# Flamingo layer on one core: pads written ahead, row scatters one tile a step, eight heads' exponentials moved to ScalarE from PSUM

## The reference

```python
def reference(x, ctx, g_xattn, g_ffn, ...):            # x: 2 x 1024 x 256, ctx: 2 x 64 x 256
    q = (layernorm(x) @ Wq + bq) / sqrt(64)            # 16 heads of 64
    k, v = ctx @ Wk + bk, ctx @ Wv + bv
    a = softmax(q @ k.T) @ v                           # per head, 64 keys
    x = x + tanh(g_xattn) * (a @ Wo + bo)
    h = layernorm(x)
    s = sigmoid(h @ W_router)                          # 8 experts
    sel = top_k(s + expert_bias, 2)
    w = s[sel] / sum(s[sel])
    shared = silu(h @ Wg_s) * (h @ Wu_s) @ Wd_s
    routed = sum over the two experts e of w_e * (silu(h @ Wg[e]) * (h @ Wu[e]) @ Wd[e])
    return x + tanh(g_ffn) * (shared + routed)
```

## Time and profile before

| | before |
|---|---|
| median of 3 runs | 332.17 us (331.71 to 333.2) |
| the profiled execution | 331.99 us, its span 330.2 us |
| mean granted TensorE clock | 0.946 of full speed |
| busy: PE, DVE, ACT, POOL | 279.2, 248.5, 153.6, 160.6 us |
| transfers | 38.01 MB; SP's queue 27.13 MB |

### The profile page before, as it was taken

One profiled execution on the slowest core, in us unless ns is written; L12 is line 12 of the kernel. 1 busy time (PEld: TensorE's weight loads), 2 busy tenths in 40 slices (PEclk: granted clock), 3 DMA queues, 4 the chain that ended last, 5 costly groups with the idle time before them and its releaser, 6 DMA issues.

```text
span 330.2 us, 6385 instructions
## 1 busy us (share of the span) xinstructions
PE 279.2 (85%) x1724; PEld 251.2 (76%) x1725; DVE 248.5 (75%) x708; ACT 153.6 (47%) x387; POOL 160.6 (49%) x208
## 2 busy tenths in 40 slices
PE   3968979999989989969968779089799999999680
PEld 2958768999979978959957667078699999999560
DVE  1696898999999998869967755028877777777666
ACT  1362455555555654635433365024456555555310
POOL 7022023355556888884788505705644443444400
PEclk9997999999999999998979999659999999999877
DMA  5792003011111232342003992232344334334668
GB/s 189 264 338 64 0 0 97 1 50 49 50 49 45 77 113 75 96 129 66 32 34 118 319 287 75 81 93 84 96 114 124 101 103 125 118 112 128 203 222 287
DMA packets 33628, 38.01 MB, mean 115 GB/s; under 512 B 3816, under 2 KB 30274, under 8 KB 33602
## 3 DMA queue, kind: packets, MB, share of 16 engines
q1 hardware_dynamic: 28018, 27.13, 27.7%
q0 software_dynamic: 3408, 8.46, 7.5%
q10 hardware_dynamic: 2176, 2.10, 1.9%
HBM read 21.67 MB, written 16.93 MB: 117 GB/s over the span
## 4 chain that ended last, share of the span: by engine, by line
PE 43%; DVE 18%; POOL 12%; issue 12%; DMA 6%; SPq 5%; ACT 2%; DVEq 0%; POOLq 0%; ACTq 0%
POOL rows_dram L556 6%; PE bank L1232 5%; PE scores_ps L1232 4%; PE bank L1233 4%; PE bank L1234 4%; PE scores_ps L1233 4%; PE scores_ps L1234 4%; DMA x_sb<-in_x_dram 3%; PE bank L1389 3%; POOL probs L585 2%; PE bank L1218 2%; DVE pT_lo L1032 2%; DVE row_sum L1037 2%; DMA routed_dram<-probs,sct_idx 2%; DVE probs L1061 2%
## 5 line engine op out<-in xcount | busy, mean ns | idle before, releaser
L638 POOL DMA_INDIRECT routed_dram<-probs,sct_idx x39 | 38.6, 991 | 56.2 <-ACT probs L804 55.1
L585 POOL TENSOR_TENSOR probs<-probs,row_inv 128x1024 f32<-128x1024 f32 x16 | 30.5, 1906 | 33.9 <-DVE row_inv L1041 33.9
L556 POOL DMA_INDIRECT rows_dram<-xn,slot_i x32 | 31.9, 997 | 20.1 <-DMA rows_dram<-pad_rows 11.5
L1232 PE MATMUL bank<-AB_hi,pT_hi 128*128 128x256 f32 x128 | 38.5, 301 | 0.0
L1234 PE MATMUL bank<-AB_hi,pT_lo 128*128 128x256 f32 x128 | 37.0, 289 | 0.0
L1233 PE MATMUL bank<-AB_lo,pT_hi 128*128 128x256 f32 x128 | 37.0, 289 | 0.0
L1232 PE MATMUL scores_ps<-AB_hi,xnT_hi 128*128 128x512 f32 x64 | 25.9, 404 | 3.4 <-DVE xnT_lo L1021 3.4
L1120 DVE TENSOR_TENSOR xnT_lo<-bank,xnT_hi 128x256 fp32r<-128x256 f32 x39 | 16.5, 424 | 14.9 <-ACT xnT_hi L789 13.7
L719 ACT ACTIVATE probs<-probs 128x1024 f32<-128x1024 f32 x16 | 16.9, 1058 | 19.0 <-DVE probs L1061 19.0
L1232 PEld LDWEIGHTS bank<-AB_hi,pT_hi 128*128 128x128 f32 x128 | 25.6, 200 | 0.0
L1233 PEld LDWEIGHTS bank<-AB_lo,pT_hi 128*128 128x128 f32 x128 | 25.6, 200 | 0.0
(11 more groups left out here) (224 smaller groups left out, 864.2 us busy)
## 6 DMA issues: line engine op xcount, KB each, us to landing
rows_dram<-pad_rows SPq DMA_DIRECT2D x8, 650.0 KB, 10.6
probs<-rows_dram SPq DMA_DIRECT2D x30, 130.0 KB, 2.2
x_sb<-in_x_dram SPq DMA_DIRECT2D x2, 1024.0 KB, 9.7
AB_free<-routed_dram SPq DMA_DIRECT2D x4, 512.0 KB, 6.3
AB_free<-routed_dram SPq DMA_DIRECT2D x8, 256.0 KB, 4.8
out_dram<-x_sb ACTq DMA_DIRECT2D x8, 256.0 KB, 2.2
raw_buf<-in_L_ffn_Wg_dram SPq DMA_DIRECT2D x8, 192.0 KB, 2.5
raw_buf<-in_L_ffn_Wu_dram SPq DMA_DIRECT2D x8, 192.0 KB, 2.7
```

The source lines that it names most:

```text
L556: nc.gpsimd.indirect_dma_start(rows_dram[:, :], bass.IndirectOffsetOnAxis(ap=slot_i[:, t, k:k + 1], axis=0), xn2[:, t % KEEP, :], None).th ...
L585: nc.gpsimd.tensor_tensor(pr, pr, row_inv[:, :].unsqueeze(2).to_broadcast([P, H, KV]), ALU.mult).then_inc(norm_done, 1)
L638: nc.gpsimd.indirect_dma_start(routed_dram[:, :], bass.IndirectOffsetOnAxis(ap=sct_idx[(k - 2) % (2 * RING)][:, 0:1], axis=0), y_sb[ks][:, ...
L1232: nc.tensor.matmul(out_ap, a_hi, b_hi, start=first, stop=False)
```

## The change

1. **Pads ahead.** Every region is now exactly 16 tiles (`REGION = T`) and is filled with pads as a whole before rows are scattered over them: the first 6 tiles of each of the 8 regions right behind the loads (`fill_first`), and one more tile of all regions with each later weight transfer (`fill_next`). Pool waits for the fill that covers the tile it scatters. Counting for the pads, `put_pads` and their semaphores are gone.
2. **Scatters.** Pool scatters one tile in each step from 6 on, right behind the second norm and ahead of the normalising; tile 9 at the end of step 14, tiles 10 and 11 in step 15.
3. **Batches** are (0,3), (3,6), (6,9), (9,12) and then as before; `rank` stands behind the scores on TensorE and `place` behind the subtraction on VectorE.
4. **Softmax.** Scores are made negative by the sign of the query weights, the maximum becomes a minimum, and for heads 0 to 7 ScalarE takes exp(-s + min) straight from PSUM with the sum in the same instruction, one instruction for each head. Heads 8 to 15 go as before, at half the width.
5. **ScalarE's order.** The experts' weight copy comes before the transposed second tile, the direct exponentials after it, Wd's copy after those; xnT_hi comes ahead of the old exponential.

```diff
-REGION = T + 1
+REGION = T
-BATCHES = [(0, 4), (4, 7), (7, 10), (10, 12), (12, 14), (14, 15), (15, 16)]
-COUNTED = 3
+BATCHES = [(0, 3), (3, 6), (6, 9), (9, 12), (12, 14), (14, 15), (15, 16)]
+FIRST = 6
...
+        def fill_first(eng):
+            eng.wait_ge(pad_ready, 3)
+            eng.dma_start(rows_dram[PAD_TILE * P:(PAD_TILE + 1) * P, :], pad_rows[:, :]).then_inc(pads_put, 16)
+            for e in range(E):
+                area = rows_dram[e * REGION * P:(e * REGION + FIRST) * P, :]
+                eng.dma_start(area.rearrange("(p r) d -> p r d", r=FIRST),
+                              pad_rows[:, :].unsqueeze(1).to_broadcast([P, FIRST, ROW])).then_inc(filled[0], 16)
+        def fill_next(eng, s):
+            areas = rows_dram[0:PAD_TILE * P, :].rearrange("(e s p) d -> s p e d", s=REGION, p=P)
+            eng.dma_start(areas[FIRST - 1 + s], pad_rows[:, :].unsqueeze(1).to_broadcast([P, E, ROW])).then_inc(filled[s], 16)
...                                                          # SP
             sp.dma_start(x_sb[:, TB:T, :], x[1].rearrange("(t p) d -> p t d", p=P)).then_inc(ld_x[1], 16)
+            fill_first(sp)
             sp.wait_ge(B_done, HP)
...
+                if e >= 2:
+                    fill_next(sp, e - 1)
...
-            put_pads(sp)
+                fill_next(sp, E - 1 + n)
...                                                          # Pool
             def put_rows(t):
+                if t == 0:
+                    pool.wait_ge(filled[0], 16 * E)
+                if t >= FIRST:
+                    pool.wait_ge(filled[t - FIRST + 1], 16)
...
                 if inside(w):
                     second_norm(w)
+                if 6 <= t < T - 1:
+                    put_tile(t - 6)
+                if t == T - 1:
+                    put_tile(10)
+                    put_tile(11)
                 if inside(m):
...
+                if t == T - 2:
+                    put_tile(9)
...
             second_norm(T - 1)
-            pool.wait_ge(pads_put, 16 * (E + 1))
-            put_batch(4)
-            put_batch(5)
-            put_batch(6)
+            for t in range(BATCHES[4][0], T):
+                put_tile(t)
...                                                          # ScalarE
-                                         scale=DH ** -0.5, bias=q_beta[:, c:c + 1]).then_inc(wqT_done, 1)
+                                         scale=-DH ** -0.5, bias=q_beta[:, c:c + 1]).then_inc(wqT_done, 1)
...
-                    nc.scalar.activation(prob[1 - q][:, :], prob[1 - q][:, :], ACT.Exp).then_inc(exp_done, 1)
+                    nc.scalar.activation(prob[1 - q][:, HK // 2:], prob[1 - q][:, HK // 2:], ACT.Exp, scale=-1.0).then_inc(exp_done, 1)
+                def direct_exponentials():
+                    act.wait_ge(max_done, u + 1)
+                    after(act, pT_done, 2 * t + 2)
+                    for h in range(H // 2):
+                        heads = slice(h * KV, (h + 1) * KV)
+                        e = nc.scalar.activation(prob[q][:, heads], scores_ps[:, heads], ACT.Exp, scale=-1.0,
+                                                 bias=neg_max[:, h:h + 1], accum_out=row_sum[:, h:h + 1])
+                    e.then_inc(direct_done, 1)
...                                                          # VectorE
-                    nc.vector.tensor_reduce(row_sum[:, :], prob[1 - q][:, :].rearrange("p (h k) -> p h k", k=KV),
+                    nc.vector.tensor_reduce(row_sum[:, H // 2:], prob[1 - q][:, HK // 2:].rearrange("p (h k) -> p h k", k=KV),
                                             AX_X, ALU.add).then_inc(sum_done, 1)
                     dve.wait_ge(sum_done, m + 1)
+                    dve.wait_ge(direct_done, m + 1)
...
-                    nc.vector.tensor_reduce(row_max[:, :], sc, AX_X, ALU.max).then_inc(max_done, 1)
+                    after(dve, direct_done, u)
+                    nc.vector.tensor_reduce(neg_max[:, :], sc, AX_X, ALU.min).then_inc(max_done, 1)
...
-                    nc.vector.tensor_tensor(prob[q][:, :].rearrange("p (h k) -> p h k", k=KV), sc,
-                                            row_max[:, :].unsqueeze(2).to_broadcast([P, H, KV]),
+                    nc.vector.tensor_tensor(prob[q][:, HK // 2:].rearrange("p (h k) -> p h k", k=KV), sc[:, H // 2:, :],
+                                            neg_max[:, H // 2:].unsqueeze(2).to_broadcast([P, H // 2, KV]),
                                             ALU.subtract).then_inc(sub_done, 1)
...                                                          # TensorE: scores
                     after(pe, sub_done, u)
+                    after(pe, direct_done, u)
```

More of the change, by code:

```diff
@@ L245, in flamingo_layer @@
         pads_put = sem("pads_put")
+        filled = [sem(f"filled{s}") for s in range(REGION - FIRST + 1)]
         tile_row_done = sem("tile_row_done")
@@ L557, in put_rows, with put_tile @@
                                                  xn2[:, t % KEEP, :], None).then_inc(rows_put[t % KEEP], 16)
-            def put_batch(b, part=slice(None)):
+            def put_tile(t):
+                b = [t < z for _, z in BATCHES].index(True)
                 pool.wait_ge(slot_done, b + 1)
                 pool.wait_ge(payload_done, b + 1)
-                for t in list(range(*BATCHES[b]))[part]:
-                    put_rows(t)
+                put_rows(t)
             def second_norm(w):
@@ L727, in step @@
                                          ACT.Copy).then_inc(xT_hi_done, 1)
+                if inside(m) and not scores_first:
+                    exponentials()
                 if folding:
@@ L1043, in step @@
                     B_low(range(HP // 2, HP))
-                for b, (_, z) in enumerate(BATCHES):
-                    if z + 2 == t:
-                        if b == COUNTED:
-                            pad_rows_at()
-                        place(b)
                 if inside(v):
@@ L1325, in step @@
                         mm.then_inc(pT_done, 1)
-                for b, (_, z) in enumerate(BATCHES):
-                    if z + 2 == t:
-                        rank(b)
-                        if b == COUNTED:
-                            count(range(*BATCHES[b]), pads_ps_done)
                 if inside(v):
@@ L1343, in step @@
                     mm.then_inc(scores_done, 1)
+                for b, (_, z) in enumerate(BATCHES):
+                    if z + 2 == t:
+                        rank(b)
                 if inside(w):
```

53 lines of the change are left out of this document (11 added, 42 removed).

## The result

The changed kernel takes **323.0 us** (median of 4 runs, 322.6 to 323.4) against 331.9 for the kernel before in the same comparison: ratio 0.9724, 95% interval 0.9695 to 0.9754. Later, in another comparison, the same file took 321.7 against 333.1, ratio 0.9665 (0.9627 to 0.9702). The forecast was 319, the range 312 to 328. So it gained 9 to 11 us where 13 were forecast.

What follows compares the result with a forecast made beforehand. TensorE's own work was taken to bound plain loop steps at 8.0 us, with loop stalls and a pads' wait before the experts. Terms: -9.1 - 2.5 - 7.75 + 4.1 + 2.2 = -13.05, from 331.99 to 319 us; range 312 to 328.

Steps and rivals of the forecast that it cites:

- A: Last second norm's shift to experts' first transpose: without the pads' wait, late shared work on TensorE limits; -9.1 us.
- B: Head of the expert loop: without the hole TensorE comes warm and runs at full clock; -2.5 us.
- C: Token loop, tile 1's to tile 13's residual add: stalls fall from 15.05 to 7.3 us; -7.75 us.
- D': Tiles 13 to 15, to the last second norm's shift: Pool is the chain, 19.9 us instead of 15.85; +4.1 us.
- E: Before the loop: tile 1's direct block ahead of xnT_hi delays tile 2's scores; +2.2 us, bounds +0.5 and +4.
- F: Pad fills, 17 MB instead of 5.3, run in a silent queue or behind weights: cost nothing, upper bound +8 us.
- D: Length of ScalarE's block of eight direct exponentials: 0.32 us each with accumulator, 2.6 us.
- the dearer accumulator: Rival: the accumulator costs its upper bound, the direct block takes 3.3 us, total about 325 us; chance 0.18.
- Pool's pace: Rival: Pool paces the token loop, 0.5 us more in eight steps, total 323 us; chance 0.10.
- plain steps: Sign: token-loop steps bound by TensorE's own work stay 8.0 us; the prediction is wrong if they change length.

Runs made afterwards that it cites:

- direct from tile 3: Changed kernel with tiles 0 to 2 in the old softmax and direct exponentials only from tile 3 on: 315.9 us, ratio 0.9492; again 317.6 us, 0.9479.
- Wd first: Changed kernel with ScalarE's copy of Wd's high half ahead of the direct exponentials in steps 10 to 13: 320.3 us, ratio 0.9582.
- ranks ahead: Changed kernel with the rank matmuls, and VectorE's part that reads them, back ahead of the scores: 320.8 us, ratio 0.9595.
- pads alone: Kernel before with only the early pad fills and the scatters' wait for them; batches, Pool's order, ranks and softmax as before: 321.2 us, ratio 0.9637.

## Why the prediction was right, and where its sizes were off

| step | forecast | measured |
|---|---|---|
| A, pads' wait | -9.1 | -7.9; -9.3 in the traces without TensorE's stop |
| B, clock | -2.5 | -0.9; -2.3 to -2.7 in four other traces, -1.3 to -1.9 in six |
| C, tiles 1 to 13 | -7.75 | -7.4 |
| D', tiles 13 to 15 | +4.1 | +4.0, +3.4 |
| E, before the loop | +2.2 | +3.0, +4.3 (clock 0.83 at 30 to 40 us) |
| F, fills | 0 | 0 |
| sum | -13.05 | -9.2 in the span |

**A** had the right mechanism: the late shared work is what is late next, 17.0 forecast, 16.6 to 16.8 measured in four kernels. What I did not see is a stop of TensorE by some 1 to 2 us between shift and last slot_i. It came in both executions of the changed kernel (9.98 and 9.93 us) and in neither of direct from tile 3 (7.99 and 7.81). But one comparison's four kernels all had it and none of the eight of two others, so it can go with the program or with the comparison and its chip; its cause is open. **B**: the granted clock was 1.00 at 216 to 224 as said, and the first 8.5 us up to Pool's first scatter of expert rows, 10.84 before, give back 2.35; VectorE's stop near 297.7 hid 1.5 of it in the profiled execution.

**C** came out right by luck: two parts are wrong and cancel. Three choosing steps exceed 8.0 by 1.4, 1.6 and 1.5, 4.5 in all, where I had 3.3 and 1.5 for their ranks, 4.8. But four such steps precede tile 13's add, not three: the fourth, step 13, exceeds by 2.4, and by 2.6 both without direct exponentials and with Wd first, so it is not ScalarE's order. That order, charged with 2.5, cost 0.8, in step 12 (8.8 us; 7.9 with Wd first, which loses 0.6 in step 10 instead). And the move of the ranks, which I read from the earlier trace rows as a wait taken away, is worth nothing, as the run with ranks ahead shows: that wait and VectorE's lateness are one delay, seen from two instructions. The loop's gain, 5.7 of 7.4, came with Pool's one tile a step and the new batches, which no run takes apart; the 12.85 us between tiles 10 and 11 are gone. **D** was 2.6 forecast and 2.3 measured. The Trainium skill, page "ScalarE: Activation LUTs", section "What ACT_TABLE_LOAD costs", gives 280 ns + 0.833 ns an element for one with a bias column, by estimate 333 ns for 64; the group of the run without accumulator has 330, so the trace agrees on the length. Less the page's overlap of 93 ns, the spacing would by the same estimate be 0.24; the trace has 0.20, and with the accumulator, which the page does not price, 0.29.

**D'** has the forecast size, and a quarter of its cause is shown. Wd's high half behind the direct block is 0.85 (Wd first). TensorE's clock, halved in step 15 after it idled for Pool, is 1.1 to 1.3; the prediction had no clock in this place. The rest is argued to be Pool's issues: pads alone, with Pool's old order, has 1.5 too, and there TensorE's clock fell in step 14. The sum also counts from the end of tile 13's attention (167.76), and the add, from which before is counted, came 1.4 later, behind the fourth choosing; so that 19.9 met 19.85 is luck. **E** is the term that was too small: the block of tile 1 does start the scores of tile 2 late (50.22 against 50.65 forecast, 48.77 before), 1.5 us, and then they ran at 1.2 GHz, 0.63 us a matmul, for another 1.5. **F** holds.

Of the rivals, the dearer accumulator and Pool's pace gave 325 and 323, near the result, but plain steps stayed 8.0 us, so neither is why. What the forecast did not ask is whether each part pays for itself. The pads alone give 0.9637; the direct exponentials, in all tiles and with the accumulator, cost more than they bring (0.9541 without them). Kept from the start of the loop they may pay (0.9492 and 0.9479; the intervals overlap with that of 0.9541, and in the trace of the latter the clock was low before the loop). Leaving out the accumulator gives as much (0.9473). These two are the fastest here; the two together were not run.

## What to carry over

When a change bundles a large gain with reorderings, sum each part by itself and ask which pays: here one did, and one cost what another brought. A wait at the head of a step and a late engine in the same step are often one delay; count it once. Where an edit makes TensorE wait 2 to 4 us, add the work behind the wait at half clock to the price, unless another engine is late there anyway. When a sum comes out right, count its steps in the trace: here a fourth choosing step stood where a wrong charge had been put.

## What the runs showed of the hardware

- After an idle time of TensorE of 3.66 us (step 0) the granted clock fell to 0.50, 1.2 GHz: a matmul of 512 columns took 0.63 instead of 0.40 us for the next few us. Sixteen matmuls that did nothing else kept it at 1.00. After about 2 us in the last steps it fell in some executions (1.84 us, changed kernel) and held in others (1.82 us, ranks ahead).
- An activation with an accumulator output is followed by an instruction of its own, 217 ns, overlapped with the next activation; the spacing rises from 0.20 to 0.29 us at 128x64.
- Fills at 286 GB/s from 28 to 48 us (pads alone) beside the four engines' work made none of their steps before tile 1's add longer: 62.47 against 62.52 us.
- A stop of TensorE of 0.7 to 2.0 us near the last slot_i (VectorE's wait there 2.3 to 3.6 us, otherwise 1.62) came in all four kernels of one comparison and in the changed kernel's first execution, and in none of eight others. No run here tells why.
